# Attention output turned in 32x32 blocks by VectorE instead of by TensorE transposes and ScalarE copies

## Chip, cores and metric

The kernel runs on 1 core of one Trainium2 chip. The metric is the device time of one execution in microseconds (us), the median of repeated runs.

## What is computed

The input x has 2 batches of 1024 tokens and 256 features. A layer norm gives xn; the result is x plus causal attention of 16 heads of 16 dimensions over xn plus a mixture of 8 experts (the two best of each token) over xn, all in float32.

```
xn = layernorm(x)
q, k, v = xn @ Wq + bq, xn @ Wk + bk, xn @ Wv + bv      # per head
y = softmax(q k^T / 4 + causal) v                        # [2, 16, 1024, 16]
attn = y.transpose(0, 2, 1, 3).reshape(2, 1024, 256) @ Wo + bo
ffn  = sum over e of w_e * ((clip(silu(xn @ Wg[e]), -7, 7) * (xn @ Wu[e])) @ Wd[e])
out = x + attn + ffn
```

## The kernel before

**Units.** Attention is done in 8 units u of 4 heads each (4 units a batch). For each unit, TensorE first makes the scores in their natural layout ("nat", line 1268), so that VectorE can take each row's maximum (lines 1004 and 1007). The negated maxima go back through a small transpose and a DMA into the packed operands, and TensorE makes the scores a second time, now with keys on partitions and the maximum already subtracted ("s", line 1287). ScalarE takes the exponent (line 896), GpSimd masks the diagonal blocks (line 823), and TensorE weighs v ("pv", `weigh_v`, line 1307): the four heads of a unit go to PSUM partitions 32h to 32h+31, of which rows 0 to 15 are the head's output, row 16 the sum of the exponents (v carries a column of ones), and tokens lie along the 512 columns of one PSUM bank. A unit has two halves c of 512 tokens, so there are 16 such banks y(u, c).

**From y(u, c) to the projection.** ScalarE copies the bank to SBUF (`copy_y`, line 906). TensorE turns it in four 128x128 transposes into another bank, with tokens on partitions (`transpose_y`, line 1316). VectorE takes the reciprocals of the sums (line 1037) and multiplies (line 1042, `normalise`), into the tile y. When all heads of a batch are there, each of its 8 token tiles t is turned back, so that features lie on partitions (`transpose_heads`, line 1325: two transposes a tile), copied by ScalarE into the double-buffered yt (line 912), and multiplied by Wo (`project`, line 1347); VectorE adds the result to x (line 1065). For the last 8 tiles (batch 1), the first 128 features are projected early, after unit 5 (`transpose_first_heads`, line 1333; copy, line 918; `project_first_heads`, line 1338; add, line 1057), and only the last 128 after unit 7. So there are 64 transposes at line 1316, 24 at line 1325 and 8 at line 1333.

**Experts.** After the routing (on VectorE, up to about 70 us), 39 tiles of 128 token slots go one by one through gather and weight fetch (GpSimd's indirect DMAs), transpose, gate and up products (line 1364), tanh on ScalarE, two products on VectorE (lines 1166 and 1169), the down product (line 1373), a ScalarE copy and a scatter. At the end the scattered rows come back (SP's `z_load`), VectorE adds them to x (lines 1049 and 1051), and SP stores x.

**Order of the work.** Nothing is scheduled at run time. `make_plan` (lines 257 on) lists every stage as a job with an engine, a cost in ns, what it comes after, a due time, and which PSUM bank it takes or frees; `Planner.run` simulates them and returns one fixed order for each engine and a bank for each fill. `walk` then emits each engine's stages in that order, so each engine executes in order and a stage that waits holds up all behind it. The due times of attention and of the experts are spread over the windows of `PACE` (line 253):

```
PACE = dict(attention=(60000, 425000), experts=(90000, 375000))
```

The limits of banks per kind are in `ROOM` (nat 3, s 3, y 2), out of 8 banks. The jobs that the change touches are in lines 385 to 415.

Of the kernel before, what the change touches and what calls it, by code (L numbers as in the profile page):

```python
# [25 lines left out]
BF16 = mybir.dt.bfloat16  # L26
# [20 lines left out]
UH = 4  # L47
# [23 lines left out]
BANKS = 8  # L71
ZS = 6
# [180 lines left out]
PACE = dict(attention=(60000, 425000), experts=(90000, 375000))  # L253


def make_plan():
# [110 lines left out]
    for g in range(NS * UNITS):  # L367
# [17 lines left out]
        if last_of_half(n):  # L385
            due = due_at[g + 1]
            before = (u, 0) if c else (u - 1, 1)
            after = [("PE", ("pv", g))] + ([("PE", ("y_t", *before))] if (u, c) > (0, 0) else [])
            job("ACT", ("y", u, c), 465, after, due - 1000, frees=("y", u, c))
            pe(("y_t", u, c), 450, [("ACT", ("y", u, c))], due, ("y_t", u, c))  # L390
            after = [("PE", ("y_t", u, c))]
            if u == 0:
                after += [("DVE", ("list",))]
            if u == G:
                after += [("PE", ("proj_t", HALF * c + HALF - 1))]
            dve(("norm", u, c), 626, after, due, ("y_t", u, c))
            tiles = range(TB * (u // G) + HALF * c, TB * (u // G) + HALF * (c + 1))
            if u == G + G // 2 - 1:
                for t in tiles:
                    pdue = due + 5000 * (t % HALF) + 5000  # L400
                    pe(("half_t", t), 110, [("DVE", ("norm", u, c))], pdue, ("half_t", t))
                    after = [("PE", ("half_t", t))] + ([("PE", ("half", t - 2))] if t >= LATE + 2 else [])
                    job("ACT", ("half_yt", t), 200, after, pdue, frees=("half_t", t))
                    pe(("half", t), 427, [("ACT", ("half_yt", t))], pdue, ("half", t))
                    dve(("half", t), 335, [("PE", ("half", t)), ("POOL", ("residual", t))], pdue, ("half", t))
            if u % G == G - 1:
                for t in tiles:
                    pdue = due + 4000 * (t % HALF) if t < LATE else due + LAST_DUE * (1 - c)
                    pe(("proj_t", t), 220 if t < LATE else 110, [("DVE", ("norm", u, c))], pdue, ("proj_t", t))
                    after = [("PE", ("proj_t", t)), ("PE", ("proj", t - 2)) if t >= 2 else ("PE", ("bias",))]  # L410
                    job("ACT", ("yt", t), 252 if t < LATE else 200, after, pdue, frees=("proj_t", t))
                    pe(("proj", t), 853 if t < LATE else 427, [("ACT", ("yt", t))], pdue, ("proj", t))
# [3 lines left out]
    for i in range(MAX_TILES):  # L416
# [14 lines left out]
        dve(("hid", i), 780, [("ACT", ("tanh", i))] + ([("PE", ("d", i - 2))] if i >= 2 else []), due + 1000, ("gu", i))  # L431
# [39 lines left out]
def build(nc, x_d, wqk_d, wvr_d, bqk_d, bv_d, wo_d, bo_d, wexp_d, out_d):  # L471
    with ExitStack() as ctx:
# [38 lines left out]
        yraw = sb("yraw", [P, BANK])  # L511
        ones_row = yraw[:, :].bitcast(BF16)
        rec = sb("rec", [P, 4, UH])
        y = sb("y", [P, TB, D])
        yt = sb("yt", [P, 2, DC, P])
# [41 lines left out]
        yt_half = xnt_flat[:, (WSLOTS - OWN_WSLOTS) * WROW:(WSLOTS - OWN_WSLOTS) * WROW + 2 * P].rearrange("p (a t) -> p a t", t=P)  # L557
# [6 lines left out]
        yo = sb("yo", [P, 2, D])  # L564
        z = stage[:, :, :, :].rearrange("p a b t -> p (a b t)").bitcast(F32).rearrange("p (r k d) -> p r k d", k=2, d=D)

        row_hot = y[:, :, :].rearrange("p t d -> p (t d)").bitcast(BF16).rearrange("p (k t r) -> p k t r", k=2, r=P)
# [35 lines left out]
        y_raw = sem("y_raw")  # L603
        rec_ready = sem("rec_ready")
        sum_step = sem("sum_step")
# [36 lines left out]
        def wait_weighed(eng, g):  # L642

            u, n = divmod(g, NS)
            if last_of_half(n):
                wait_filled(eng, ("y", u, STEPS[n][0]))
            else:
                eng.wait_ge(pv_done, pv_counted(g))

# [181 lines left out]
        def _(act):  # L831
# [67 lines left out]
            def copy_y(u, c):  # L899

                bank = wait_filled(act, ("y", u, c))
                if u == c == 0:
                    act.wait_ge(ones_in, 16)
                else:
                    wait_filled(act, ("y_t", *divmod(2 * u + c - 1, 2)))
                act.copy(yraw[:, :], psum[:, bank, :]).then_inc(freed[bank], 1)

            def copy_yt(t):
                bank = wait_filled(act, ("proj_t", t))
                wait_filled(act, ("proj", t - 2) if t >= 2 else ("bias",))  # L910
                c = 0 if t < LATE else DC - 1
                act.copy(yt[:, t % 2, c:DC, :], psum[:, bank, P * c:D].rearrange("p (a t) -> p a t", t=P)).then_inc(freed[bank], 1)

            def copy_yt_half(t):
                bank = wait_filled(act, ("half_t", t))
                if t >= LATE + 2:
                    wait_filled(act, ("half", t - 2))
                act.copy(yt_half[:, t % 2, :], psum[:, bank, 0:P]).then_inc(freed[bank], 1)

# [13 lines left out]
            def copy_yo(i):  # L933
                bank = wait_filled(act, ("d", i))
                if i >= 2:
# [4 lines left out]
                         "y": copy_y, "yt": copy_yt, "half_yt": copy_yt_half, "xgt": copy_xgt, "tanh": silu_gate, "yo": copy_yo})  # L940
# [3 lines left out]
        def _(dve):  # L944
# [39 lines left out]
            def widen_v_bias():  # L984

                dve.wait_ge(wvr_in, 32)
                dve.tensor_copy(yt[:, 0, :, :], bv[:, :].unsqueeze(2).to_broadcast([P, DC, P])).then_inc(bias_wide, 1)
# [44 lines left out]

            def normalise(u, c):

                bank = wait_filled(dve, ("y_t", u, c))
                part = psum[:, bank, :].rearrange("p (t h w) -> p t h w", t=4, h=UH)
                chain(rec_ready, dve.reciprocal(rec[:, :, :], part[:, :, :, HD]))
                g = u % G
                if u == G:
                    wait_filled(dve, ("proj_t", HALF * c + HALF - 1))  # L1040
                dst = y[:, 4 * c:4 * c + 4, UH * HD * g:UH * HD * (g + 1)].rearrange("p t (h w) -> p t h w", h=UH)
                dve.tensor_tensor(dst, part[:, :, :, 0:HD], rec[:, :, :].unsqueeze(3).to_broadcast([P, 4, UH, HD]),
                                  ALU.mult).then_inc(freed[bank], 1)
# [117 lines left out]
            def hidden(i):  # L1161
                bank, _ = FILL_AT[("gu", i)]
                dve.wait_ge(tanh_ready, i + 1)
                if i >= 2:
# [10 lines left out]
                         "bias": add_bias, "max": row_max, "negate": negate_max, "neg": copy_neg, "norm": normalise,  # L1175
# [4 lines left out]
        def _(pe):  # L1180
# [72 lines left out]
            def project_bias():  # L1253
# [3 lines left out]
                for c in range(DC):  # L1257
                    ins = pe.matmul(psum[:, bank, 0:D], yt[:, 0, c, :], wo[:, c, :], start=c == 0, stop=c == DC - 1)
# [53 lines left out]
            def transpose_y(u, c):  # L1312
                wait_freed(pe, ("y", u, c))
                bank, full = wait_room(pe, ("y_t", u, c))
                for t in range(4):
                    ins = pe.transpose(psum[:, bank, P * t:P * (t + 1)], yraw[:, P * t:P * (t + 1)], ident[:, :])  # L1316
                ins.then_inc(full, 1)

            def transpose_heads(t):

                if t % HALF == 0:
                    wait_freed(pe, ("y_t", G * (t // TB) + G - 1, t // HALF % 2))
                bank, full = wait_room(pe, ("proj_t", t))
                for c in range(DC) if t < LATE else (DC - 1,):
                    ins = pe.transpose(psum[:, bank, P * c:P * (c + 1)], y[:, t % TB, P * c:P * (c + 1)], ident[:, :])
# [104 lines left out]
```

## Time and profile before

| | |
|---|---|
| median of 3 runs | 441.3 us (441.29 to 441.75) |
| span of the profiled execution (first to last instruction) | 440.0 us |
| the profiled execution with what lies around its span, taken as the run nearest to it | 441.3 us |
| TensorE busy | 422.0 us (96%), 2851 matmuls |
| VectorE busy | 314.2 us (71%) |
| ScalarE busy | 237.6 us (54%) |
| GpSimd busy | 194.6 us (44%) |
| granted TensorE clock, mean | 0.984 |

The profile gives times in us and means in ns. Matmuls are pipelined: the duration of one runs until its last result is written, while the next one has already started, so the distance between starts is shorter than the duration. A row of a group reads: line, engine, operation, written from read, shapes, count, then busy time and mean ns of one, then the engine's idle time before them and what ended it. A row of a table by stretch reads: stretch, its length, busy time (and count) of PE (TensorE), PEld (its weight loads), DVE (VectorE), ACT (ScalarE) and POOL (GpSimd), then the granted clock, the DMA share and GB/s.

### The profile page before, as it was taken

The numbers are of one execution on the slowest core, as the hardware profiler recorded it, in microseconds if no ns is written. First come the engines' busy times: TensorE is split into PE (matmuls) and PEld (weight loads), VectorE is DVE, ScalarE is ACT, GpSimd is POOL, SyncE is SP. The second block draws the span as 40 slices with busy tenths as digits, with TensorE's granted clock in tenths as the row PEclk, the third lists the DMA queues.
The fourth block names the chain that finished last, engine by engine and source line by source line (L and its number), as shares of the span: only waits on it lengthen the run. The fifth ranks groups of instructions, "written<-read, shape, count | busy, mean of one in ns | idle before, by whom it ended". The sixth has DMA issues, their size and how long they took to land.

```text
span 440.0 us, 8430 instructions
## 1 busy us (share of the span) xinstructions
PE 422.0 (96%) x2851; PEld 255.2 (58%) x2851; DVE 314.2 (71%) x1019; ACT 237.6 (54%) x551; POOL 194.6 (44%) x223
## 2 busy tenths in 40 slices
PE   8898979989999999999999999999999999999896
PEld 8486425656364366557666676565655664756333
DVE  6827999999888835885577735867576768591485
ACT  1563363433647665655564546646555547464992
POOL 5331256585054277346744256233743365212410
PEclk9999959998999999999999999999999999999999
DMA  7289896788076249435784069621893454110582
GB/s 237 70 218 201 277 207 182 257 280 269 4 150 181 83 135 230 154 118 187 184 233 175 23 187 221 189 87 50 245 256 107 145 155 153 21 38 3 169 310 97
DMA packets 40373, 71.34 MB, mean 162 GB/s; under 512 B 5893, under 2 KB 30598, under 8 KB 40332
## 3 DMA queue, kind: packets, MB, share of 16 engines
q0 software_dynamic: 9360, 39.99, 28.8%
q1 hardware_dynamic: 27132, 26.76, 24.5%
q10 hardware_dynamic: 3840, 4.08, 3.6%
q8 instruction: 23, 0.38, 0.4%
q14 instruction: 18, 0.15, 0.1%
HBM read 55.85 MB, written 15.60 MB: 162 GB/s over the span
## 4 chain that ended last, share of the span: by engine, by line
PE 72%; DVE 18%; issue 3%; DMA 3%; POOL 2%; ACT 1%; SPq 0%; ACTq 0%
PE psum L1364 15%; PE psum L1307 14%; PE psum L1268 11%; PE psum L1287 11%; PE psum L1373 7%; DVE psum L1004 5%; DVE mxa L1007 5%; PE psum L1223 3%; PE psum L1199 3%; PE psum L1347 2%; DMA bqk<-in_bqk 2%; PE psum L1316 2%; PE psum L1354 2%; DVE resid L976 1%; POOL probs L823 1%
## 5 line engine op out<-in xcount | busy, mean ns | idle before, releaser
L896 ACT ACTIVATE probs<-psum 128x512 f32<-128x512 f32 (+1 forms) x320 | 151.5, 575 | 38.6 <-PE psum L1287 37.8
L1004 DVE CUSTOM_DVE_ANT_0 psum<-psum,maskrow 128x128 f32<-128x128 f32 (+3 forms) x256 | 121.4, 505 | 18.1 <-PE psum L1268 17.8
L1268 PE MATMUL psum<-packk,packq 96*128 96x512 bf16 (+3 forms) x384 | 93.3, 328 | 2.5 <-DVE mxa L1004 1.2
L1007 DVE TENSOR_REDUCE mxa<-psum 128x1 f32<-128x512 f32 x128 | 87.7, 685 | 9.4 <-PE psum L1268 9.2
L1287 PE MATMUL psum<-packq,packk 99*128 99x512 bf16 (+3 forms) x384 | 90.5, 332 | 2.9 <-ACT probs L896 2.7
L1307 PE MATMUL psum<-probs,v 128*32 128x512 f32 (+3 forms) x768 | 76.1, 502 | 2.2 <-POOL probs L823 1.8
L823 POOL TENSOR_SCALAR_AFFINE_SELECT probs<-probs 128x512 f32<-128x512 f32 (+1 forms) x48 | 40.0, 836 | 64.1 <-ACT probs L896 63.6
L1268 PEld LDWEIGHTS psum<-packk,packq 96*128 96x128 bf16 x384 | 34.5, 97 | 54.7 <-issue 16.8
L1287 PEld LDWEIGHTS psum<-packq,packk 99*128 99x128 bf16 x384 | 33.0, 98 | 45.1 <-issue 12.7
L790 POOL DMA_INDIRECT xg<-xn_rows,token x39 | 37.6, 965 | 45.9 <-PE psum L1354 35.9
L1166 DVE SCALAR_TENSOR_TENSOR tanh<-tanh,psum 128x256 f32<-128x256 f32 x39 | 16.3, 417 | 49.8 <-ACT tanh L931 49.5
L931 ACT ACTIVATE tanh<-psum 128x256 f32<-128x256 f32 x39 | 14.9, 383 | 66.1 <-PE psum L1364 66.1
L808 POOL DMA_INDIRECT expert_rows<-yo,slots x39 | 39.3, 1008 | 24.3 <-ACT yo L937 13.1
L1364 PEld LDWEIGHTS psum<-xgt,wexp 128*128 128x128 f32 x384 | 45.4, 192 | 4.1 <-issue 3.4
L1364 PE MATMUL psum<-xgt,wexp 128*128 128x128 f32 x384 | 47.5, 277 | 0.1
L802 POOL DMA_INDIRECT wexp<-in_wexp,wrow x24 | 23.2, 967 | 44.7 <-PE psum L1373 38.3
L1307 PEld LDWEIGHTS psum<-probs,v 128*32 128x32 f32 x768 | 19.3, 109 | 28.4 <-issue 21.2
L776 POOL TENSOR_TENSOR stage<-resid,stage 128x512 bf16<-128x512 f32 x16 | 19.8, 1248 | 32.8 <-ACT stage L874 32.7
L1199 PE MATMUL psum<-xnt,wqk 128*128 128x512 f32 x64 | 30.6, 595 | 1.6 <-DMA bqk<-in_bqk 1.6
L1364 PEld LDWEIGHTS psum<-xgt,xnt 128*128 128x128 f32 x240 | 30.3, 201 | 1.5 <-issue 0.9
L1364 PE MATMUL psum<-xgt,xnt 128*128 128x128 f32 x240 | 30.9, 284 | 0.3 <-ACT xgt L924 0.2
L937 ACT ACTIVATE yo<-psum 128x256 f32<-128x256 f32 x39 | 15.2, 391 | 29.3 <-PE psum L1373 29.1
(127 smaller groups left out, 477.2 us busy)
## 6 DMA issues: line engine op xcount, KB each, us to landing
qk_parts<-stage SPq DMA_DIRECT2D x24, 256.0 KB, 2.9
stage<-expert_rows SPq DMA_DIRECT2D x16, 256.0 KB, 4.1
packq<-qk_parts SPq DMA_DIRECT2D x16, 192.0 KB, 4.6
packk<-qk_parts SPq DMA_DIRECT2D x14, 192.0 KB, 6.1
x<-in_x SPq DMA_DIRECT2D x4, 512.0 KB, 5.3
packq<-qk_parts SPq DMA_DIRECT2D x16, 128.0 KB, 6.2
xn_rows<-probs ACTq DMA_DIRECT2D x4, 512.0 KB, 14.5
out<-x SPq DMA_DIRECT2D x16, 128.0 KB, 2.5
```

The lines of the kernel that those rows point to most:

```text
L790: pool.indirect_dma_start(out=xg[:, i % 2, :], out_offset=None, in_=xn_d, in_offset=bass.IndirectOffsetOnAxis(ap=token[:, i:i + 1], axis=0))\
L808: pool.indirect_dma_start(out=z_d, out_offset=bass.IndirectOffsetOnAxis(ap=slots[:, i:i + 1], axis=0), in_=yo[:, i % 2, :], in_offset=None ...
L823: pool.affine_select(out=cols, in_=cols, compare_op=ALU.is_ge, fill=0.0, base=0, pattern=pattern, channel_multiplier=-1).then_inc(probs_ma ...
L896: act.activation(probs[:, g % RING, h, 0:width], psum[:, bank, 0:width], ACT.Exp, scale=SCALE)\
L1004: ins = dve.tensor_tensor_reduce(out=chunk, in0=chunk, in1=maskrow[:, BANK - width:], scale=1.0, scalar=NEG, op0=ALU.add, op1=ALU.max, acc ...
L1007: ins = dve.tensor_reduce(into, chunk, op=ALU.max, axis=AX.X)
L1199: return pe.matmul(psum[:, bank, :], wqk[:, op, c, P * grp:P * (grp + 1)], xnt_moe[:, c, cols], start=c == 0, stop=c == DC - 1)
L1268: pe.matmul(psum[:, bank, 0:width], packq[0:MAXROW, u % SLOTS, i // HALF, h, P * (i % HALF):P * (i % HALF + 1)], packk[0:MAXROW, u % SLOTS ...
L1287: ins = pe.matmul(psum[:, bank, at:at + width], packk[0:KROWS, u % SLOTS, j // HALF, h, P * (j % HALF):P * (j % HALF + 1)], packq[0:KROWS, ...
L1307: ins = pe.matmul(psum[32 * h:32 * h + 32, bank, t0:BANK], v[:, TB * b + j, at:at + 32], probs[:, g % RING, h, begin:begin + width], start ...
L1364: ins = pe.matmul(psum[:, bank, P * m:P * (m + 1)], wexp[i % WSLOTS][:, at:at + P], xgt[:, i % 2, c, :], start=c == 0, stop=c == DC - 1)
L1373: ins = pe.matmul(psum[:, bank, 0:D], hid[:, i % 2, P * c:P * (c + 1)], wexp[i % WSLOTS][:, at:at + D], start=c == 0, stop=c == DC - 1)
```

## The change

The bank y(u, c) is read by VectorE itself: one `transpose` turns each 32x32 block of the 128x512 bank into yblk (`token_blocks`). A block holds one head (32 rows: 16 dimensions, the sum, padding) and 32 tokens, so afterwards the tokens of a block lie on 32 partitions and the head's rows along 32 columns. `normalise` takes 16 reciprocals per partition and multiplies into ypair, in which each block of 32 columns has room for the 16 dimensions of two heads: an even unit fills columns 0 to 15, the odd unit after it columns 16 to 31. After the odd unit a second 32x32 transpose turns ypair into yt, with features on partitions and tokens along columns, which is the operand that the projection needs. yt is now [128, 2, 1024], held for all tokens. The features come in another order (heads of two units side by side), so the rows of Wo and the bias of v are permuted on the host (`pairs`).

With this, `copy_y`, `transpose_y`, `copy_yt`, `transpose_heads`, `copy_yt_half` and `transpose_first_heads` are gone, together with their banks. `project` and `project_first_heads` wait once per four tiles for a new semaphore that VectorE raises after the second transpose. SBUF is laid out anew: the widened bias of v lies in hid's space, so that the first expert's `hidden` comes after the bias sum; yo lies in the space of the weights wvr, row_hot in yt's. In the plan, `PACE` changes, the jobs of the removed stages are gone, "blocks" costs 620 and "norm" 680 or 1320 on VectorE, and VectorE's norm of unit 5 (`u == G + 1`) waits for the projections of batch 0, where that of unit 4 waited for batch 0's transposes.

```diff
-PACE = dict(attention=(60000, 425000), experts=(90000, 375000))
+PACE = dict(attention=(60000, 410000), experts=(90000, 360000))
...
         if last_of_half(n):
             due = due_at[g + 1]
-            before = (u, 0) if c else (u - 1, 1)
-            after = [("PE", ("pv", g))] + ([("PE", ("y_t", *before))] if (u, c) > (0, 0) else [])
-            job("ACT", ("y", u, c), 465, after, due - 1000, frees=("y", u, c))
-            pe(("y_t", u, c), 450, [("ACT", ("y", u, c))], due, ("y_t", u, c))
-            after = [("PE", ("y_t", u, c))]
-            if u == 0:
+            pair = u % 2
+            after = [("PE", ("pv", g))] + ([("DVE", ("norm", *((u, 0) if c else (u - 1, 1))))] if (u, c) > (0, 0) else [])
+            dve(("blocks", u, c), 620, after, due - 1000, ("y", u, c))
+            after = [("DVE", ("blocks", u, c))]
+            if u == 1:
                 after += [("DVE", ("list",))]
-            if u == G:
-                after += [("PE", ("proj_t", HALF * c + HALF - 1))]
-            dve(("norm", u, c), 626, after, due, ("y_t", u, c))
+            if u == G + 1:
+                after += [("PE", ("proj", HALF * c + HALF - 1))]
+            dve(("norm", u, c), 1320 if pair else 680, after, due - 1000)
...
-        yraw = sb("yraw", [P, BANK])
-        rec = sb("rec", [P, 4, UH])
-        y = sb("y", [P, TB, D])
-        yt = sb("yt", [P, 2, DC, P])
+        yblk = sb("yblk", [P, BANK])
+        rec = sb("rec", [P, BANK // QUAD])
+        ypair = sb("ypair", [P, 2, BANK])
+        yt = sb("yt", [P, DC, T])
...
+            def token_blocks(u, c):
+                if u == c == 0:
+                    dve.wait_ge(ones_in, 16)
+                bank = wait_filled(dve, ("y", u, c))
+                dve.transpose(yblk[:, :], psum[:, bank, :]).then_inc(freed[bank], 1)
+
             def normalise(u, c):
...
+                wait_freed(dve, ("y", u, c))
+                part = yblk[:, :].rearrange("p (b w) -> p b w", w=QUAD)
+                chain(rec_ready, dve.reciprocal(rec[:, :], part[:, :, HD]))
+                pair = u % 2
+                dst = ypair[:, c, :].rearrange("p (b w) -> p b w", w=QUAD)[:, :, HD * pair:HD * (pair + 1)]
+                chain(rec_ready, dve.tensor_tensor(dst, part[:, :, 0:HD],
+                                                   rec[:, :].unsqueeze(2).to_broadcast([P, BANK // QUAD, HD]), ALU.mult))
+                if pair:
+                    if u == G + 1:
+                        wait_filled(dve, ("proj", HALF * c + HALF - 1))
+                    dve.transpose(yt[:, u % G // 2, BANK * c:BANK * (c + 1)], ypair[:, c, :]).then_inc(heads_ready, 1)
...
             def project(t):
                 if t == 0:
                     pe.wait_ge(wo_in, 32)
-                wait_freed(pe, ("proj_t", t))
+                if t % HALF == 0:
+                    wait_heads(pe, G * (t // TB) + G - 1, t // HALF % 2)
                 bank, full = wait_room(pe, ("proj", t))
                 chunks = range(DC) if t < LATE else (DC - 1,)
                 for c in chunks:
-                    ins = pe.matmul(psum[:, bank, 0:D], yt[:, t % 2, c, :], wo[:, c, :], start=c == chunks[0], stop=c == DC - 1)
+                    ins = pe.matmul(psum[:, bank, 0:D], yt[:, c, P * (t % TB):P * (t % TB + 1)], wo[:, c, :],
+                                    start=c == chunks[0], stop=c == DC - 1)
```

## Rows read from the trace of the kernel before

**Rows 1.** Busy time by engine in five stretches, whole kernel.

```profile
44.00:110.00 66.00, 60.98 (x338) 34.27 (x336) 63.94 (x194) 27.53 (x55) 37.92 (x35) 0.90 0.82 246
110.00:405.00 295.00, 292.66 (x2100) 178.10 (x2098) 202.66 (x659) 166.81 (x386) 134.23 (x148) 1.00 0.50 138
405.00:431.60 26.60, 25.03 (x205) 10.46 (x201) 15.75 (x36) 23.64 (x55) 7.85 (x10) 1.00 0.60 202
431.60:440.00 8.40, 4.38 (x20) 2.78 (x20) 5.00 (x13) 1.55 (x5) 0.00 (x0) 0.96 0.34 113
sum 440.00, PE 421.95 PEld 255.25 DVE 314.17 ACT 237.56 POOL 194.63; mean PE 84.39 PEld 51.05 DVE 62.83 ACT 47.51 POOL 38.93
```

**Rows 2.** Chain that ended last, by line, from 44 to 110 us.

```profile
by line: DVE psum L1004 18.5%; DVE mxa L1007 16.9%; DVE resid L976 8.3%; PE psum L1364 8.1%; issue 6.9%; DVE y L1119 6.7%; DVE wexp L1126 4.3%; PE psum L1199 3.9%; PE psum L1268 2.0%; DVE mxb L1004 1.9%; DVE topi L1077 1.7%; DVE wexp L1129 
```

**Rows 3.** The same from 110 to 405 us.

```profile
by line: PE psum L1364 20.4%; PE psum L1307 18.5%; PE psum L1268 16.2%; PE psum L1287 14.3%; PE psum L1373 10.0%; DVE psum L1004 3.3%; DVE mxa L1007 3.1%; PE psum L1347 2.5%; PE psum L1354 2.4%; PE psum L1316 2.0%; PE psum L1338 1.1%; issue
```

**Rows 4.** The same from 405 to 431 us.

```profile
by line: PE psum L1307 34.6%; PE psum L1287 20.9%; POOL probs L823 10.7%; ACT probs L896 10.1%; issue 6.4%; PE psum L1316 4.8%; PE psum L1347 4.1%; POOL expert_rows L808 3.8%; ACT yraw L906 2.3%; DVE x L1049 1.9%; PE psum L1325 1.7%; ACT yt
```

**Rows 5.** Groups of instructions by line: the steps that leave, and two VectorE products.

```profile
L1316 PE MATMUL psum<-ident,yraw 128*128 128x128 f32 x64 | 9.9, 278 | 0.1
...
L906 ACT COPY yraw<-psum 128x512 f32<-128x512 f32 x16 | 9.4, 585 | 14.7 <-PE psum L1307 14.5
...
L1051 DVE SCALAR_TENSOR_TENSOR x<-stage,gate,x 128x256 f32<-128x256 f32 x16 | 7.8, 485 | 0.6
...
L1042 DVE TENSOR_TENSOR y<-psum,rec 128x256 f32<-128x256 f32 x16 | 6.8, 424 | 0.6
...
L1325 PE MATMUL psum<-ident,y 128*128 128x128 f32 x24 | 4.3, 275 | 1.3 <-DVE y L1042 1.3
...
L1333 PE MATMUL psum<-ident,y 128*128 128x128 f32 x8 | 2.2, 279 | 0.0
```

**Rows 6.** Timeline of TensorE, 128 to 130 us (start, us, instruction).

```profile
128.12 0.60 PE L1316 MATMUL psum<-ident,yraw 128*128 128x128 f32 x4
128.56 0.60 PE L1268 MATMUL psum<-packk,packq 96*128 96x384 bf16 x3
```

**Rows 7.** Timeline of TensorE, 269 to 270.5 us.

```profile
269.12 0.66 PE L1316 MATMUL psum<-ident,yraw 128*128 128x128 f32 x4
269.62 1.03 PE L1373 MATMUL psum<-wexp,hid 128*128 128x256 f32 x4
```

**Rows 8.** Line 1316 alone, the stretch from 110 to 405 us.

```profile
110.00:405.00 295.00, 7.43 (x48) 5.50 (x48) 1.00 0.50 138
```

**Rows 9.** Timeline of VectorE, 71 to 76 us.

```profile
71.96 0.68 DVE L1007 TENSOR_REDUCE mxa<-psum 128x1 f32<-128x512 f32 x1
72.56 0.68 DVE L1004 CUSTOM_DVE_ANT_0 psum<-psum,maskrow 128x512 f32<-128x512 f32 x1
```

**Rows 10.** Line 1169, the second half of the SiLU step on VectorE.

```profile
L1169 DVE SCALAR_TENSOR_TENSOR hid<-tanh,psum x39: 420/420/423, 86.5 to 405.1; 128x256 f32<-128x256 f32 x39
```

**Rows 11.** Chain that ended last, 405 to 440 us (start, us, what).

```profile
411.34 0.59 ACT yraw L906
411.98 0.66 PE psum L1316 x4
```

**Rows 12.** Timeline of the last 16 us, all engines.

```profile
431.64 0.59 ACT L906 COPY yraw<-psum 128x512 f32<-128x512 f32 x1 [0.77 <-PE psum L1307]
...
433.64 0.25 DVE L1037 RECIPROCAL rec<-psum 128x16 f32<-128x16 f32 x1
433.92 0.42 DVE L1042 TENSOR_TENSOR y<-psum,rec 128x256 f32<-128x256 f32 x1
...
434.40 0.66 PE L1325 MATMUL psum<-ident,y 128*128 128x128 f32 x4 [1.32 <-DVE y L1042]
...
435.08 2.24 PE L1347 MATMUL psum<-wo,yt 128*128 128x256 f32 x8
```

**Rows 13.** Timeline of TensorE, 234 to 237 us.

```profile
234.74 1.89 PE L1347 MATMUL psum<-wo,yt 128*128 128x256 f32 x8
```

More of the change, by code:

```diff
@@ L71 @@
 BANKS = 8
+QUAD = 32
 ZS = 6
@@ L400, in make_plan @@
                     pdue = due + 5000 * (t % HALF) + 5000
[L401 to L404, printed above, removed]
+                    pe(("half", t), 427, [("DVE", ("norm", u, c))], pdue, ("half", t))
                     dve(("half", t), 335, [("PE", ("half", t)), ("POOL", ("residual", t))], pdue, ("half", t))
@@ L408, in make_plan @@
                     pdue = due + 4000 * (t % HALF) if t < LATE else due + LAST_DUE * (1 - c)
[L409 to L412, printed above, removed]
+                    pe(("proj", t), 853 if t < LATE else 427, [("DVE", ("norm", u, c))], pdue, ("proj", t))
                     after = [("PE", ("proj", t)), ("POOL", ("residual", t))]
@@ L430, in make_plan @@
         job("ACT", ("tanh", i), 280, [("PE", ("gu", i))] + ([("DVE", ("hid", i - 2))] if i >= 2 else []), due + 1000)
-        dve(("hid", i), 780, [("ACT", ("tanh", i))] + ([("PE", ("d", i - 2))] if i >= 2 else []), due + 1000, ("gu", i))
+        dve(("hid", i), 780, [("ACT", ("tanh", i))] + ([] if i else [("DVE", ("bias",))]) + ([("PE", ("d", i - 2))] if i >= 2 else []), due + 1000, ("gu", i))
         pe(("d", i), 853, [("DVE", ("hid", i))], due + 2000, ("d", i))
@@ L648, in wait_weighed, with wait_heads @@
                 eng.wait_ge(pv_done, pv_counted(g))
+        def wait_heads(eng, u, c):
+            eng.wait_ge(heads_ready, 2 * (u // 2) + c + 1)
         def walk(engine, stages):
@@ L897, in exps @@
                    .then_inc(freed[bank], 1)
[L899 to L918, printed above, removed]
             def copy_xgt(i):
@@ L1257, in project_bias @@
                 for c in range(DC):
-                    ins = pe.matmul(psum[:, bank, 0:D], yt[:, 0, c, :], wo[:, c, :], start=c == 0, stop=c == DC - 1)
+                    ins = pe.matmul(psum[:, bank, 0:D], bvw[:, c, :], wo[:, c, :], start=c == 0, stop=c == DC - 1)
                 ins.then_inc(full, 1)
@@ L1310, in weigh_v, with project_first_heads @@
                 ins.then_inc(filled[bank] if last else pv_done, 1)
[L1312 to L1319, printed above, removed]
-                if t % HALF == 0:
[L1322 to L1325, printed above, removed]
-                ins.then_inc(full, 1)
-            def transpose_first_heads(t):
-                if t % HALF == 0:
-                    wait_freed(pe, ("y_t", G + G // 2 - 1, t // HALF % 2))
-                bank, full = wait_room(pe, ("half_t", t))
-                pe.transpose(psum[:, bank, 0:P], y[:, t % TB, 0:P], ident[:, :]).then_inc(full, 1)
-            def project_first_heads(t):
-                wait_freed(pe, ("half_t", t))
+            def project_first_heads(t):
+                if t % HALF == 0:
+                    wait_heads(pe, G + G // 2 - 1, t // HALF % 2)
                 bank, full = wait_room(pe, ("half", t))
-                pe.matmul(psum[:, bank, 0:D], yt_half[:, t % 2, :], wo[:, 0, :], start=True, stop=True).then_inc(full, 1)
+                pe.matmul(psum[:, bank, 0:D], yt[:, 0, P * (t % TB):P * (t % TB + 1)], wo[:, 0, :], start=True, stop=True).then_inc(full, 1)
             def project(t):
```

33 lines of the change are left out of this document (13 added, 20 removed).

## Prediction

> **What bounds the kernel now.** I read the table by stretch first, cut where the work changes: routing and the first unit up to 110 us, the even middle up to 405, then the end without experts [rows 1]. The reader is to see which engine is full in which stretch. From 44 to 110 us VectorE is busy 63.9 of 66.0 us and TensorE 61.0, with a granted clock of 0.90. From 110 to 405 us TensorE is busy 292.7 of 295.0 and VectorE only 202.7. From 405 to 431.6 us TensorE has 25.0 and ScalarE 23.6 of 26.6. In the last 8.4 us TensorE has 4.4. Then the chain of waits of each stretch, since a busy share alone doesn't say who waits for whom. Up to 110 us its largest parts are VectorE's row maxima and residues (lines 1004, 1007, 976: 18.5, 16.9 and 8.3%) [rows 2]. From 110 to 405 us it is nearly all TensorE, and line 1316, which the change removes, has 2.0% of it [rows 3]. From 405 to 431 us TensorE's score and weighing products alternate with ScalarE and GpSimd, and the ScalarE copy (line 906, 2.3%) and the transposes (lines 1316 and 1325, 4.8 and 1.7%) are links [rows 4]. So a TensorE instruction is worth its place in the middle, a VectorE instruction costs in the early stretch, and at the end the length of the handoffs counts.
>
> **What the transposes cost TensorE.** The table of groups gives 9.9, 4.3 and 2.2 us of busy time to lines 1316, 1325 and 1333, 16.4 us in all, for 64, 24 and 8 transposes with means of 275 to 279 ns [rows 5]. I don't take this for the price, because the engine starts the next matmul before the last one has ended. The timeline shows it: a group of four starts at 128.12 and the next line at 128.56, so four hold the engine 0.44 us, 0.11 each [rows 6]; a group at 269.12 is followed at 269.62, 0.50 us [rows 7]. Taken: 0.50 for a group of four at line 1316, 0.11 for a single one; low end 0.11 each throughout, high end the busy times. Part by part:
>
> **Middle, 110 to 405 us.** 48 of the 64 transposes of line 1316 lie here, with 7.43 us of busy time [rows 8]; that is 12 groups, 12 x 0.50 = 6.0 us. Of lines 1325 and 1333 16 (batch 0) and 8 lie here: 24 x 0.12 = 2.9 us. TensorE idles 295.0 - 292.7 = 2.3 us, so nothing else bounds the stretch and all of it counts: -8.9 us. Low end 72 x 0.11 = 7.9; high end 7.4 + 4.3 x 16/24 + 2.2 = 12.5.
> ScalarE loses its copies here, which gains nothing: it has 128 us of idle time.
> VectorE gains work. No transpose of VectorE stands in the trace. Its nearest rows are one-bank reads of PSUM: a reduce of 128x512 starts at 71.96, the next instruction at 72.56, so 0.60 us each, with durations of 0.68 [rows 9]. I take 0.60 for either transpose, with 0.5 as the cheap end and two passes, 1.36, as the dear end. There are 16 + 8 = 24, 14.4 us. The multiply of `normalise` reads SBUF instead of PSUM: 424 ns becomes at most the 485 of line 1051, which reads SBUF too [rows 5], 16 x 0.06 = 1.0 us. VectorE goes from 314 to 330 us of about 428, 77%; in the middle about 12 + 6 transposes and 12 multiplies, 11.5 us, come into 92 us of idle time, so at nothing. If that cover went, they would cost 11.5.
>
> The Trainium skill, VectorE: DVE Perf Modes, The three transpose paths, has 311 ns for a VectorE transpose of 128x128 in bf16; four of these are 1.24 us a bank, within my ends. No run here shows it yet. By it the early stretch and the final chain below would each lose more, 0.6 and 1.1 us, and the sum would come to 431.1.
>
> **The waits that move.** `copy_y` waited for pv on ScalarE, 14.5 us in all [rows 5]. Now `token_blocks` waits there on VectorE. Behind it in VectorE's queue stand row maxima, the SiLU products and the projection's adds; TensorE waits for the row maxima through the three banks that "nat" may hold. In exchange VectorE no longer waits for TensorE's transposes before the reciprocal. The planner places the stage where it expects pv to be done, as it did before for the reciprocal. I count nothing, and keep it as a rival. The new wait of norm(5, c) for the projection of batch 0 replaces one on its transposes one unit earlier, with slack of a unit. `hidden` of the first tile now comes after the bias sum; it starts at 86.5 us [rows 10], when the bias product, planned for 30 us, is long over: nothing. No DMA and no SP or GpSimd stage is moved, only their due times with `PACE`.
>
> **Early stretch, up to 110 us.** One of the 16 groups lies here. VectorE sets this stretch, so TensorE's 0.5 us bring nothing, and one transpose and one slower multiply, 0.6 + 0.1, cost: +0.7 us (0.5 to 1.4).
>
> **End with pv, 405 to 431.6 us.** Two y's lie here. At the first, the chain runs through the copy, 411.34 and 0.59 us, and the transposes, 411.98 and 0.66 [rows 11]: 1.25 us. For the second, the transposes are on the chain [rows 4], 0.6 us; four single ones of line 1325 add 4 x 0.11. Sum -2.3 us (0 to -2.3, since another engine's chain runs beside it: ScalarE is busy 23.6 of 26.6 us, and loses 1.2 us of copies).
>
> **Final chain.** The last pv is done just before 431.64, when the copy starts; transposes, reciprocal at 433.64, multiply at 433.92, transposes at 434.40, first projection at 435.08: 3.44 us [rows 12]. After: transpose 0.68, reciprocal 0.28 (distance of the starts), multiply 0.48, transpose 0.68, handoffs of 0.1 each twice: 2.3 us. That is -1.1. The eight matmuls of the last four projections now take 2.24 us, held up by two yt buffers [rows 12]; with all operands ready they should take the 1.89 of line 1347 at 234.74 [rows 13]: -0.3. Sum -1.4 us (-2 to +0.5, if VectorE's additions of expert rows stand ahead of both transposes or these are dear).
>
> **Sum.** -8.9 + 0.7 - 2.3 - 1.4 = -11.9 us. The profiled execution has a span of 440.0 us; no time of its own is given, and 1.3 us around the span make it 441.3, which is also the median of the runs shown. 441.3 - 11.9 = 429.4 us. What is late next: TensorE still, at 96%.
>
> **Rivals.** (a) TensorE's drop is larger: the busy times of the groups are the price, and the freed banks let score products start earlier. 12.5 instead of 8.9 in the middle, and up to 2 us out of TensorE's 5 us of idle time up to 110 us: 441.3 - 17.5 = 424. For it speaks that the planner rebuilds the order with less bank traffic; against it rows 6. Chance 0.16.
> (b) The gain is partly lost. VectorE's 15 us, its waits for pv, or an end that ScalarE's exponents set (23.6 of 26.6 us) give back 5 to 6 us: 435. A longer low clock is in this case too: from 44 to 110 us the mean granted clock is 0.90 [rows 1], which is some 13 us at the lower level, 1.2 GHz, and as much again where TensorE is full would cost about 6 us. For it: the new order isn't known, and VectorE is full up to 110 us. Chance 0.20.
> (c) The wait moved to VectorE decides, the other side. In place and price: `token_blocks` inherits the 14.5 us in which ScalarE waited, the row maxima stop behind it, and once three "nat" banks are full TensorE, in order, stops too. If none is covered, 429.4 + 14.5 = 443.9 us. It decides from the point at which TensorE's new idle time passes 11.9 us. Against it: VectorE runs ahead with 92 us to spare in the middle, and the planner knows the job. Chance 0.06; somewhat covered, it lands near no change, 0.03.
> (d) Each transpose held TensorE for its whole duration: 96 x 0.277 = 26.6 us, so 441.3 - 26.6 + 0.7 - 1.2 = 414. The starts 0.11 apart contradict it [rows 6]. Chance 0.01. The Trainium skill, TensorE: Matmul & The Clock Gate, Part 4: PE-mode transpose, gives about 275 ns for a transpose in a kernel's context; the trace agrees with that as a duration, not as the time that it takes from others.
> That the change doesn't do what it says I exclude: the removed stages are out of the order.
>
> **How the numbers follow.** The forecast, -9 to -14.5 us, has 0.54; (a) 0.16, (b) 0.20, (c) 0.06, near no change 0.03, (d) 0.01. The predicted time is the forecast's, 429.4 us. The range from 423.5 to 437.0 takes in the forecast, the greater part of (a) and (b), and leaves out (c), (d) and the outer ends, under 2 in 10. About 0.2%, 0.9 us, is what a measurement of this kernel tells from no change; faster by more: 0.54 + 0.16 + 0.20 + 0.01 = 0.91, less 0.01 for the edge of (b), 0.90; within it 0.03; slower 0.07.
>
> **What would show it.** TensorE's matmuls fall by 96 to 2755 and its busy time to about 410 us, still over 95% of the span. Two new groups of VectorE transposes, 16 and 8, at about 0.68 us each; if they show 1.3, the early stretch and the final chain are worse. VectorE's busy time near 330 us, ScalarE's near 221. In the middle, TensorE's idle time still near 2 us: if it is 5 or more, with VectorE as the releaser and `token_blocks` waiting for pv, (b) or (c) holds. Last pv to first projection 2.3 us. The prediction is wrong if TensorE's idle time grows by over 5 us, or if the clock falls for longer.

## Result, and the profile after

| | before | after |
|---|---|---|
| median of the runs | 441.5 us (4 runs, 441.29 to 441.75) | 438.48 us (4 runs, 438.36 to 439.29) |
| ratio to before | | 0.9927, 95% interval 0.99 to 0.9954 |
| span of the profiled execution | 440.0 us | 436.4 us |
| matmuls; TensorE busy | 2851; 422.0 us | 2755; 412.3 us |
| VectorE busy | 314.2 us | 332.0 us |
| ScalarE busy | 237.6 us | 222.4 us |

The change is faster by 3.0 us where 11.9 were forecast, and lies outside the range, which ended at 437.0. The sign was right, the size a quarter.

The first part of the page of the changed kernel:

```profile
span 436.4 us, 8151 instructions
...
PE 412.3 (94%) x2755; PEld 246.4 (56%) x2755; DVE 332.0 (76%) x1043; ACT 222.4 (51%) x511; POOL 196.5 (45%) x223
```

TensorE's busy time fell by 9.7 us, near the forecast, but the span of the profiled execution by 3.6 only: its idle time grew from 18.1 to 24.1 us, past the 5 us that the prediction named as a sign of being wrong. The groups of instructions (line, engine, operation, shapes, count, then busy us, mean ns, idle before):

```profile
L1312 PE MATMUL psum<-wo,yt 128*128 128x256 f32 x48 | 14.1, 430 | 4.9 <-DVE yt L1029 4.9
...
L1015 DVE STREAM_TRANSPOSE yblk<-psum 128x512 f32<-128x512 f32 x16 | 11.5, 716 | 18.6 <-PE psum L1293 18.4 <-issue 0.2
...
L1024 DVE TENSOR_TENSOR ypair<-yblk,rec 128x256 f32<-128x256 f32 x16 | 6.9, 432 | 0.5
...
L1029 DVE STREAM_TRANSPOSE yt<-ypair 128x512 f32<-128x512 f32 x8 | 5.7, 711 | 0.3
```

The two transposes (the "turns" from here on) stand in the place of lines 906, 1316, 1325 and 1333 of [rows 5], and the multiply in that of line 1042. The 24 turns take 716 and 711 ns each, 17.2 us busy; the multiply takes 432 ns, against 424 from PSUM. The projection, line 1312 (line 1347 before), has a mean of 430 ns where the profile before had 394: some of its matmuls ran at a lower clock, and TensorE idled 4.9 us just before it. The table by stretch, cut where the last weighing of v ends (425.2 us, before 431.6) and where the even middle ends:

```profile
44.00:110.00 66.00, 59.51 (x337) 32.04 (x335) 64.06 (x195) 28.17 (x57) 38.91 (x35) 0.95 0.81 246
110.00:400.00 290.00, 284.58 (x2021) 171.77 (x2020) 216.41 (x677) 154.32 (x355) 133.49 (x146) 0.99 0.51 141
400.00:425.20 25.20, 24.39 (x198) 9.40 (x197) 18.35 (x38) 21.92 (x50) 9.47 (x11) 1.00 0.69 220
425.20:436.40 11.20, 3.78 (x9) 2.52 (x8) 6.29 (x14) 0.00 (x0) 0.00 (x0) 0.62 0.21 70
sum 436.40, PE 412.30 PEld 246.44 DVE 332.03 ACT 222.45 POOL 196.51; mean PE 82.46 PEld 49.29 DVE 66.41 ACT 44.49 POOL 39.30
```

The last stretch is the plainest. It took 8.4 us before [rows 1] and takes 11.2 now, at a granted clock of 0.62. The middle has 5.4 us of idle time in 290, where it had 2.3 in 295 before. Up to 110 us the clock is 0.95, where it was 0.90, so the time at the lower level is shorter there, not longer. What the early stretch cost, forecast as +0.7, can't be told from these rows, since the two orders differ in it. The list of TensorE's own waits names two places:

```profile
PE psum L1312 <- DVE yt L1029: 4.9, 1, 4.9
PE psum L1320 <- DMA xg<-xn_rows,token: 3.3, 1, 3.3
```

**The first, at 209 us.** The timeline of TensorE around it:

```profile
207.68 1.03 PE L1339 MATMUL psum<-xnt,hid 128*128 128x256 f32 x4
211.97 0.44 PE L1320 MATMUL psum<-ident,xg 128*128 128x128 f32 x2 [3.26 <-DMA xg<-xn_rows,token]
212.34 1.08 PE L1293 MATMUL psum<-probs,v 128*32 128x256 f32 x16
```

TensorE ends its work at 208.7 us and gets the rows of the next expert tile (tile 15) at 211.97. They come from a gather that GpSimd issued at 205.17:

```profile
205.17 0.97 POOL L788 DMA_INDIRECT xg<-xn_rows,token  x1 [0.30 <-issue]
```

Just then SP issues the twelve pack loads of unit 5, 1.5 MB; the first and the last of them:

```profile
204.84 0.40 SPq L691 DMA_DIRECT2D packq<-qk_parts  x1
...
210.08 0.43 SPq L691 DMA_DIRECT2D packk<-qk_parts  x1
```

The table of that place (columns as above: granted clock, DMA share, GB/s at the end) shows the DMA engines full (shares 1.00 to 1.13), TensorE idle, and after that a clock of 0.59, which is 3.4 us at the lower level of 1.2 GHz:

```profile
205.00:209.00 4.00, 3.71 (x30) 3.25 (x28) 1.51 (x4) 1.20 (x4) 3.63 (x4) 1.00 1.00 303
209.00:213.00 4.00, 1.03 (x18) 0.65 (x18) 0.17 (x1) 0.50 (x2) 2.10 (x3) 0.98 1.12 197
213.00:217.00 4.00, 4.00 (x24) 3.30 (x17) 1.40 (x3) 0.38 (x1) 0.36 (x1) 0.59 1.13 204
```

**The second, at the end.** The last weighing starts its last instructions at 424.34 and ends at 425.2; the last four projections start at 430.06:

```profile
424.34 0.86 PE L1293 MATMUL psum<-probs,v 128*32 128x256 f32 x16 [0.21 <-POOL probs L821]
430.06 3.78 PE L1312 MATMUL psum<-wo,yt 128*128 128x256 f32 x8 [4.86 <-DVE yt L1029]
```

In between is VectorE's queue:

```profile
425.06 0.47 DVE L1035 SCALAR_TENSOR_TENSOR x<-stage,gate,x 128x256 f32<-128x256 f32 x1
425.57 0.48 DVE L1037 SCALAR_TENSOR_TENSOR x<-stage,gate,x 128x256 f32<-128x256 f32 x1
...
427.40 0.48 DVE L1037 SCALAR_TENSOR_TENSOR x<-stage,gate,x 128x256 f32<-128x256 f32 x1
427.80 0.71 DVE L1015 STREAM_TRANSPOSE yblk<-psum 128x512 f32<-128x512 f32 x1
428.55 0.25 DVE L1021 RECIPROCAL rec<-yblk 128x16 f32<-128x16 f32 x1
428.83 0.42 DVE L1024 TENSOR_TENSOR ypair<-yblk,rec 128x256 f32<-128x256 f32 x1
429.29 0.71 DVE L1029 STREAM_TRANSPOSE yt<-ypair 128x512 f32<-128x512 f32 x1
431.32 0.42 DVE L1051 TENSOR_TENSOR x<-psum,x 128x256 f32<-128x256 f32 x1 [1.31 <-PE psum L1312]
```

Three sums of expert rows (lines 1035 and 1037, six instructions from 425.06 to 427.88) stand ahead of the last turn, so 2.6 us pass between the weighing and the turn. The chain proper, from 427.80 to 430.06, is 2.26 us. In the kernel before, the same three sums stood at the same place, and the copy (431.64) and the transposes ran beside them on other engines:

```profile
430.89 0.48 DVE L1049 SCALAR_TENSOR_TENSOR x<-stage,gate,x 128x256 f32<-128x256 f32 x1
...
432.48 0.60 PE L1316 MATMUL psum<-ident,yraw 128*128 128x128 f32 x4
...
433.23 0.48 DVE L1051 SCALAR_TENSOR_TENSOR x<-stage,gate,x 128x256 f32<-128x256 f32 x1
```

The transposes were done at 433.08, and the reciprocal started at 433.64 [rows 12], when VectorE was through with the sums. In the changed kernel the eight matmuls then take 3.78 us where 1.89 do [rows 13], since the clock fell to half at 427.9 us, 2.7 us after the last weighing, and stayed there to the end. The table by stretch, cut there:

```profile
424.00:427.90 3.90, 0.99 (x17) 0.50 (x16) 3.79 (x10) 0.00 (x0) 0.20 (x1) 1.00 0.21 71
427.90:436.40 8.50, 3.78 (x8) 2.52 (x8) 3.70 (x8) 0.00 (x0) 0.00 (x0) 0.50 0.18 62
```

### The profile page after: what moved, and what is told of

It is laid out like the page before. It is cut to its first block, busy times and chain, and to the rows that moved or that the text cites. A ratio compares the mean times of both kernels' runs of the same rounds, so it can differ in the third digit from the quotient of the medians.

```text
span 436.4 us, 8151 instructions
## 1 busy us (share of the span) xinstructions
PE 412.3 (94%) x2755; PEld 246.4 (56%) x2755; DVE 332.0 (76%) x1043; ACT 222.4 (51%) x511; POOL 196.5 (45%) x223
## 4 chain that ended last, share of the span: by engine, by line
PE 68%; DVE 21%; DMA 4%; issue 4%; ACT 1%; POOL 1%; SPq 0%; ACTq 0%; DVEq 0%; POOLq 0%
PE psum L1293 14%; PE psum L1330 14%; PE psum L1254 11%; PE psum L1273 11%; PE psum L1339 8%; DVE psum L981 7%; DVE mxa L984 4%; PE psum L1209 3%; PE psum L1185 3%; PE psum L1312 3%; DMA bqk<-in_bqk 2%; PE psum L1320 2%; DMA xg<-xn_rows,token 2%; DVE resid L953 1%; DMA x<-in_x 1%
## 5 line engine op out<-in xcount | busy, mean ns | idle before, releaser
L821 POOL TENSOR_SCALAR_AFFINE_SELECT probs<-probs 128x512 f32<-128x512 f32 (+1 forms) x48 | 41.2, 863 | 44.8 <-ACT probs L894 44.7
L1273 PEld LDWEIGHTS psum<-packq,packk 99*128 99x128 bf16 x384 | 33.4, 98 | 42.7 <-issue 10.5
L806 POOL DMA_INDIRECT expert_rows<-wvr,slots x39 | 39.3, 1008 | 31.8 <-ACT wvr L914 17.2
L914 ACT ACTIVATE wvr<-psum 128x256 f32<-128x256 f32 x39 | 15.1, 388 | 43.4 <-PE psum L1339 43.3
L1330 PEld LDWEIGHTS psum<-xgt,xnt 128*128 128x128 f32 x240 | 28.3, 192 | 2.7 <-issue 2.2
L1330 PE MATMUL psum<-xgt,xnt 128*128 128x128 f32 x240 | 29.4, 277 | 0.3 <-issue 0.2
```

The source lines that it names most:

```text
L806: pool.indirect_dma_start(out=z_d, out_offset=bass.IndirectOffsetOnAxis(ap=slots[:, i:i + 1], axis=0), in_=yo[:, i % 2, :], in_offset=None ...
L821: pool.affine_select(out=cols, in_=cols, compare_op=ALU.is_ge, fill=0.0, base=0, pattern=pattern, channel_multiplier=-1).then_inc(probs_ma ...
L1273: ins = pe.matmul(psum[:, bank, at:at + width], packk[0:KROWS, u % SLOTS, j // HALF, h, P * (j % HALF):P * (j % HALF + 1)], packq[0:KROWS, ...
L1330: ins = pe.matmul(psum[:, bank, P * m:P * (m + 1)], wexp[i % WSLOTS][:, at:at + P], xgt[:, i % 2, c, :], start=c == 0, stop=c == DC - 1)
```

## Experiments

**Theory 1**, formed from the two traces: the prices of single instructions were right (a transpose of TensorE and a turn of VectorE), VectorE's new work is hidden in the middle, and the missing gain lies in two places, the gather at 209 us and the last turn behind the sums. Its **rival**: VectorE's 17 us, in order with the row maxima, cost a good part of their length all over. The kernel before was timed again beside each batch (441.2 to 441.6 us); differences below are to it in the same batch, and "the change alone" is its -3.0 us.

### Was the transpose's price right?

Each removed transpose issued twice, in the kernel before (the same for lines 1325 and 1333):

```diff
-                for t in range(4):
+                for t in (0, 0, 1, 1, 2, 2, 3, 3):
                     ins = pe.transpose(psum[:, bank, P * t:P * (t + 1)], yraw[:, P * t:P * (t + 1)], ident[:, :])
```

> The kernel before, in its own order, with each of the 96 transposes that the change removes issued twice. Theory 1 (TensorE sets the time from 110 us on, and a transpose holds it for 0.11 us): 96 x 0.11 = 10.5 us more, less the 0.4 us of the four in the early stretch and up to 1 us at the end where other engines lead: +9 to +10.5 us. Rival (the removed transposes were worth little, because other engines set the pace): +5 us or less. If a transpose were worth its full duration: +26 us.

450.44 us, ratio 1.0197 (1.0161 to 1.0233): +9.2 us. 96 transposes at 0.11 us are 10.5, so nearly all of it counts, and the full duration (26 us) is out. TensorE was the bound. Since the order is that of before, the same instruction can be followed from trace to trace, and this gives the price in the middle:

```profile
394.57 1.92 PE L1307 MATMUL psum<-probs,v 128*32 128x512 f32 x16
```

```profile
402.31 1.92 PE L1307 MATMUL psum<-probs,v 128*32 128x512 f32 x16
```

These sixteen matmuls start 7.7 us later than before; those at 112.59 us start 0.5 us later (113.11). So the 72 transposes in between cost 7.2 us, 0.10 each. The prediction's 8.9 us for them, 0.12 each, was 1.7 too much, if what is doubled costs the same as what is taken away; doubling doesn't show whether a whole group that leaves takes a switch with it.

### Was VectorE's work hidden?

The 24 turns added to the kernel before, beside what it does; yo was laid over the weights wvr to make room:

```diff
                 chain(rec_ready, dve.reciprocal(rec[:, :, :], part[:, :, :, HD]))
                 g = u % G
+                for _ in range(1 + u % 2):
+                    chain(rec_ready, dve.transpose(extra[:, :], psum[:, bank, :]))
```

> The kernel before, in its own order, with VectorE's 24 turns of 128x512 added beside what it does (one in each normalise, a second in odd units), into a tile that nobody reads. The turns are 0.72 us each in the trace of the changed kernel, 17 us in all. Theory 1 (VectorE's added work is hidden but for the early stretch and the final chain): 0.7 us early and 1.5 us in the last normalise, +1 to +3 us. Rival (VectorE's added 17 us, in order with the row maxima, cost a good part of their length, and this ate the gain): +6 us or more.

452.46 us, ratio 1.026 (1.0216 to 1.0304): +11.2 us. Theory 1 fell for this order and the rival held. Followed as above, the weighing at 394.57 us starts 7.3 us late (401.86), and the one at 113.9 us 0.3 us early: 18 turns, 12.9 us of VectorE work put where VectorE had 92 us to spare, cost 7.6. Nearly 3 us more come after the last weighing. TensorE's waits from 110 to 400 us name y as what it waited for (the kernel before waits there for VectorE once, for 0.2 us; lines are those of this kernel, three further down):

```profile
PE psum L1290 <- DVE y L1045: 1.8, 2, 1.4
PE psum L1328 <- DVE y L1045: 1.2, 1, 1.2
PE psum L1271 <- DVE y L1045: 1.1, 1, 1.1
```

To part the way to y from the mere occupancy, the same turns were issued after the multiply and from Wo, so that nothing waits for their result:

```diff
                 dve.tensor_tensor(dst, part[:, :, :, 0:HD], rec[:, :, :].unsqueeze(3).to_broadcast([P, 4, UH, HD]),
                                   ALU.mult).then_inc(freed[bank], 1)
+                for _ in range(1 + u % 2):
+                    chain(rec_ready, dve.transpose(extra[:, :], wo[:, :, :].rearrange("p c d -> p (c d)")))
```

> The kernel before, in its own order, with the same 24 turns of VectorE as in the run that cost 11.2 us, but issued after the multiply of each normalise, from Wo, so that neither y nor its bank waits for them. Theory 3 (those 11.2 us were the path from the weighing to y, on which TensorE waits in a fixed order, and not VectorE's occupancy): +1 to +4 us. Rival (VectorE's queue time itself costs, since the row maxima stand behind it): +8 us or more, as before.

447.79 us, ratio 1.0172 (1.0125 to 1.0218): +6.2 us, between the two. Both have a part: 5 us were the way to y and its bank, 6 us the occupancy. In the middle alone the 18 turns cost 4.9 here, where they cost 7.6. In the middle TensorE now waits for row maxima (mxb), which stand behind the turns:

```profile
PE psum L1271 <- DVE mxb L1005: 1.7, 2, 1.5
PE psum L1328 <- DVE mxb L1005: 1.3, 1, 1.3
```

Then the same kernel, with the length of the turns told to the planner, which makes the order around them:

```diff
-            dve(("norm", u, c), 626, after, due, ("y_t", u, c))
+            dve(("norm", u, c), 2050 if u % 2 else 1340, after, due, ("y_t", u, c))
```

> The kernel before with the 24 turns off the path of y, as in the run that cost 6.2 us, but now with their length told to the planner (normalise costs 1340 or 2050 ns in the plan instead of 626), so that the order is made around them. Theory 4 (VectorE's occupancy cost 6.2 us because the order didn't allow for it, and a planned order hides it, as the changed kernel's does in the middle): +3 us or less over the kernel before. Rival (the occupancy costs the same in any order): +5 us or more. An order differs from the next by some 2 us by itself.

443.48 us, ratio 1.0042 (1.0028 to 1.0057): +2.1 us, and 4.1 less than with the same instructions in the old order, which is about twice what one order differs from the next (below). In the middle TensorE's waits for VectorE, 4.1 us in the run before this one, are gone but for two of 0.2 us; its longest are these (the profiled execution is the slowest of the five, 445.17 us):

```profile
PE psum L1310 <- POOL probs L824: 0.5, 1, 0.5
PE psum L1367 <- issue: 0.3, 1, 0.3
PE psum L1271 <- DVE mxa L1008: 0.2, 1, 0.2
```

So VectorE's idle time covers new work if the static order is made for it; inserted into a finished order, a third of the work (6.2 of 17 us) or two thirds (11.2) shows. The change plans its stages with their lengths, and its middle shows no wait for VectorE above 0.2 us either.

### The two places of the changed kernel

SP's loads of unit 5 put behind the transposes of tile 15:

```diff
                 if u >= SLOTS:
                     wait_filled(sp, ("s", NS * (u - SLOTS + 1) - 1, UH - 1))
+                if (u, c, r) == (5, 0, 0):
+                    wait_filled(sp, ("x", 15))
```

> The changed kernel with one wait added on SP: the pack loads of unit 5 start after TensorE's transposes of expert tile 15, so that the gather of tile 15 has the DMA engines without them. Theory 1 (the gather was held up by these loads; TensorE stood 3.3 us and then ran 3.4 us at half clock): the stall and the dip go, -3 to -5 us. Rival (the gather is late by the weight fetches on its own queue): the stall stays, within 1 us.

434.01 us, ratio 0.9824 (0.9789 to 0.9859): 7.2 us under before, 4.2 more than the change alone. The gather issued at 205.83 now serves TensorE at 210.08, in 4.2 us instead of 6.8, and the clock stays at 1.00 with the DMA share down. TensorE's wait is 2.5 us shorter, and 3.4 us at half the clock had cost 1.7: these are the 4.2.

```profile
205.83 0.98 POOL L790 DMA_INDIRECT xg<-xn_rows,token  x1 [0.30 <-issue]
...
210.08 0.44 PE L1322 MATMUL psum<-ident,xg 128*128 128x128 f32 x2 [0.72 <-DMA xg<-xn_rows,token]
```

```profile
205.00:209.00 4.00, 4.00 (x36) 3.90 (x34) 0.90 (x3) 1.59 (x5) 3.52 (x4) 1.00 0.78 257
209.00:213.00 4.00, 3.28 (x32) 2.29 (x31) 2.18 (x5) 1.14 (x3) 2.75 (x4) 1.00 0.47 118
213.00:217.00 4.00, 4.00 (x26) 2.29 (x24) 2.62 (x11) 2.82 (x7) 2.81 (x3) 1.00 1.05 293
```

The rival, that the gather was late by the weight fetches on its own queue, fell: these were left as they were, and the stall went.

The sums 13 to 15 put behind the last normalise in the plan:

```diff
+FIRST_LAST = 13
...
-        dve(("sum", t), 912, after, m1 + 1000 * t)
+        dve(("sum", t), 912, after + ([("DVE", ("norm", UNITS - 1, 1))] if t == FIRST_LAST else []), m1 + 1000 * t)
```

> The changed kernel with VectorE's sums of the expert rows 13 to 15 planned behind the last normalise (7, 1); all else is as planned before. Theory 1 (the last turn waited 2.6 us behind three sums, and TensorE's idle time let the clock fall for the last four projections, 3.8 us where 1.9 are needed): the turn starts at once after the last weighing, -2.5 us, and -4.5 us if the clock stays up. Rival (the sums only move behind and the adds then wait for them): within 0.5 us of the changed kernel.

436.69 us, ratio 0.9891 (0.9855 to 0.9928): 4.5 us under before, 1.5 more than the change alone. Right in kind, less than expected. The timeline of its end shows why:

```profile
424.86 0.86 PE L1294 MATMUL psum<-probs,v 128*32 128x256 f32 x16 [0.21 <-POOL probs L822]
...
425.78 0.72 DVE L1016 STREAM_TRANSPOSE yblk<-psum 128x512 f32<-128x512 f32 x1
...
427.91 0.44 DVE L1036 SCALAR_TENSOR_TENSOR x<-stage,gate,x 128x256 f32<-128x256 f32 x1
...
428.04 2.90 PE L1313 MATMUL psum<-wo,yt 128*128 128x256 f32 x8 [2.32 <-DVE yt L1030]
...
430.62 1.41 DVE L1052 TENSOR_TENSOR x<-psum,x 128x256 f32<-128x256 f32 x4
```

The turn starts at once at 425.78 and the projections 2.3 us after it, 2.0 us sooner than in the changed kernel. But the three sums now end at 430.70, and the four adds, which need them, run behind them back to back: VectorE's own work after the last weighing, 2.1 + 2.8 + 1.4 us, is the bound. The clock fell here too, so that the eight matmuls took 2.90 us.

Both edits together:

> The changed kernel with both mends at once: SP's pack loads of unit 5 behind the transposes of expert tile 15, and the sums 13 to 15 behind the last normalise. Theory 1 (two places hold the lost time, and they are independent): -4.5 and -1.8 us add up, 432.2 us, 9 us under the kernel before, near the forecast for the transposes alone. Rival (time won at one place is lost at the next): 433.5 us or more.

432.04 us, ratio 0.9791 (0.9768 to 0.9814): 9.6 us under before, and 6.6 more than the change alone, where the two edits had brought 4.2 and 1.5 by themselves. So they add up at least, and it is the fastest version run. Its middle has 3.3 us of idle time in 290:

```profile
110.00:400.00 290.00, 286.74 (x2045) 172.47 (x2044) 216.75 (x678) 158.48 (x366) 136.39 (x150) 1.00 0.50 141
```

### The due times

The kernel after with the due times of before, and the kernel before with those of after; each edit is this line, one way or the other:

```diff
-PACE = dict(attention=(60000, 410000), experts=(90000, 360000))
+PACE = dict(attention=(60000, 425000), experts=(90000, 375000))
```

> The changed kernel with the due times of before (PACE 425000 and 375000), nothing else. Theory 1 (the stall at 209 us comes from one order among many, and the order comes from the due times): another order without this stall, so 434 us, the time that the order without the stall has; the last turn still waits behind sums. Rival (the tighter pacing is part of the gain): slower than 438.5, 440 or more.

436.69 us, ratio 0.989 (0.9873 to 0.9906): 4.9 us under before, and 1.9 more than with the new due times. No stall at 209 us. The expected 434 was not met, as TensorE waits 5.6 us for the last turn in this order.

> The kernel before with the due times of the change (PACE 410000 and 360000), nothing else. If the pacing alone is worth something to it, 439 or less; if orders differ by chance only, 441 with 2 us either way. Theory 1 expects 440 to 443.

439.22 us, ratio 0.9952 (0.9935 to 0.9968): the kernel before gains 2.4 us from the new due times alone. So the same two numbers help one kernel and hurt the other, by about 2 us. I take that as the size by which one order differs from the next; the expected 440 to 443 was too high.

This also says what the removed steps are worth by themselves, with the due times equal on both sides: 4.9 us with the old ones and 0.6 with the new ones (3.0 less 2.4), where the gather stalls. With both edits it is 7.2 us (9.6 less 2.4). So of the 9.6 us, 2.4 could be had without any change of engine.

The kernel after with both this line and the sums put last:

> The changed kernel with the due times of before and the sums 13 to 15 behind the last normalise. Theory 1 (the last turn's place in VectorE's queue costs in whatever order the rest is): about 2 to 4 us under the 436.7 of the same due times without it, 433 to 434.5. Rival (that gain belonged to the one order in which it was found): within 0.7 us of 436.7.

434.48 us, ratio 0.9851 (0.9824 to 0.9877): 7.0 us under before with equal due times, 2.0 more than the old due times alone, at the low end of what was expected. The cost of the last turn's place in the queue isn't bound to one order.

## Why the prediction was wrong

**Held.** TensorE bounds the middle, and a transpose costs it a tenth of a microsecond and not its duration of 0.28; TensorE's busy time 412.3, forecast about 410; VectorE 332, forecast 330; ScalarE 222, forecast 221; the turn 0.72 us long, taken as 0.68 in the final chain; the chain from turn to projection 2.26 us, forecast 2.3. The estimate of 1.24 us for a bank, worked out from the 311 ns that the Trainium skill, VectorE: DVE Perf Modes, The three transpose paths, has for 128x128 in bf16, doesn't hold for one instruction over a float32 bank: it took 0.716 us, so the sum by it, 431.1 us, has a wrong term as well.

**The step that failed first: "Final chain", -1.4 us.** It was +2.8: from the last weighing to the end of the span 8.4 us became 11.2. The step took 3.44 us, from ScalarE's copy to the first projection, as the length of copy, transposes and multiply, and put the turn in their place with handoffs of 0.1 us. But the copy and the transposes, 1.2 us of work, had run beside VectorE's three sums, which set the start of the reciprocal; the turn runs behind the same sums, and waits 2.6 us for them. So the way from the last weighing to the first projection grew from 3.5 to 4.9 us instead of falling by 1.1. The prediction had this only as the bound "+0.5" of that step, and did not price TensorE's clock: it fell in the gap of 4.9 us, and the last projections took 3.78 us where the step had 1.89 (and the kernel before 2.24). These two, 2.5 and 1.9 us, are the 4.2 between forecast and result within 0.2. The early start of the turn (e3_last_turn_before_sums) gave back 1.5 us.

**The step that failed second: "No DMA is moved, only due times".** The order is made anew from these, and that moved a gather next to twelve loads. To the last weighing the forecast was -10.5 us and the result -6.4, and the one wait on SP gives back 4.2. That this closes the gap is partly luck: the kernel before gains 2.4 us from the new due times alone, a term that the prediction put at nothing, and the removed steps brought less than forecast. With equal due times the last weighing ends 9.0 us earlier with the old ones (422.6 against 431.6) and 7.5 with the new ones and the mended gather (421.7 against 429.2), not 10.5.

**A term that was too large: "12 x 0.50 = 6.0" and "24 x 0.12 = 2.9", -8.9 us.** Doubling the same 72 transposes cost 7.2 us, under the low end of 7.9.

**The rivals.** The prediction had rival (b), a gain partly lost to VectorE, ScalarE or a longer low clock, 435 us: right in kind, with another cause, and 3 us short. It had no rival in which a new order meets a DMA stall, though the whole order was bound to change. The plan allows 1.25 us for the issue of a gather and 2.2 us for its landing, and counts larger transfers ahead of it; from the issue to TensorE's start it took 6.8.

**Not tested by the result, and wrong in its reason: "In the middle ... they come into 92 us of idle time, so at nothing."** In the changed kernel it cost nothing that shows. But idle time alone wasn't the reason: the same turns in the old order cost 7.6 and 4.9 us in the middle. An order made with their length was. Rival (c), that the moved wait decides, fell: `token_blocks` waited 18.4 us for the weighing in all, and TensorE's waits in the middle didn't follow.

With both mends the kernel is at 432.0 us, 2.6 from the forecast. Of that, the last four adds behind the sums are seen (8.9 us from the last weighing to the end in both runs of this order of sums, 7.0 forecast). The remaining 0.7 are no proof of the rest of the sum, since the 2.4 us of the due times are in them: by itself the change is worth 7.2 us there, not 11.9. To the last weighing the 10.5 us of the sum were 1.5 too much with the old due times and 3.0 with the new ones. The transposes' 1.7 cover the first and half of the second; what the other half is stays open.

## What to carry to other kernels

Moving a step from idle engines to another engine's queue is priced by what stands ahead of it there at the moment it becomes critical, above all at the end, where queues hold the epilogue; look at the rows of that queue, not at its busy share. In a kernel whose order is fixed ahead, idle time on an engine covers new work only if the order is made around it, and remaking the order moves everything else by some 2 us either way: look for new collisions, such as a gather beside large loads, before crediting or blaming the change, and time the old kernel with the new planning numbers too. Two such places, each mended by an edit of a line or two, held 6.6 of the 9 us that were missing here.

## Unexpected of the hardware

- VectorE's 32x32 block transpose of a 128x512 float32 bank takes 0.716 us from PSUM and 0.711 us from SBUF, the duration of other one-bank instructions (0.68 to 0.74).
- TensorE could start on the rows of a 128 KB gather 6.8 us after its issue beside 1.5 MB or so of loads and a weight fetch (DMA share 1.12), and 4.2 us after it with the loads held back until it had landed.
- After TensorE had stood for 3.3 us at 209 us, the granted clock was at the lower level for 3.4 us; after a gap of 4.9 us at the end it stayed there for the last projections, which took 3.78 us instead of 1.89. In the three runs with the sums last the gaps were 2.3, 2.3 and 3.0 us, and the same matmuls took 2.90, 3.36 and 2.51 us, so the gap's length alone doesn't tell what the clock costs.
